# Masked cross attention: the barred keys are added by VectorE in its search for the maximum, GpSimd turns the sign, and the loop is written out

## The reference

```python
q = (layernorm(x) @ wq.T + bq) / sqrt(16);  k = ctx @ wk.T + bk;  v = ctx @ wv.T + bv    # per head: 112 x 16, 375 x 16
last_key = cumsum(steps)                       # per batch, one number for each of the 112 queries
scores = q @ k.T                               # 112 x 375 for each head
scores = where(key_index > last_key, barred, scores)
probs = softmax(scores);  x = x + (probs @ v) @ wo.T + bo
```

## Time and profile before

| | us |
|---|---|
| median of three runs | 3923.49 (3920.95 to 3923.75) |
| the profiled execution | 3921.66, its span 3919.8 |
| TensorE busy in the span | 3269.5 (83%) |
| VectorE, ScalarE, GpSimd busy | 1619.4 (41%), 1577.4 (40%), 1254.9 (32%) |
| DMA | 287.81 MB, 73 GB/s over the span |
| mean granted TensorE clock | 0.92 of full speed |

### The profile page before, as it was taken

The page is one execution under the profiler, slowest core; times in us unless marked ns, Lnnn a source line. Parts: engine busy times, 40 slices in busy tenths (PEclk is TensorE's granted clock), DMA queues, the critical chain, the costliest instruction groups (busy, mean ns, idle before and its releaser), DMA issues. The chain is left out here.

```text
span 3919.8 us, 67890 instructions
## 1 busy us (share of the span) xinstructions
PE 3269.5 (83%) x22398; PEld 2797.8 (71%) x22398; DVE 1619.4 (41%) x3595; ACT 1577.4 (40%) x4385; POOL 1254.9 (32%) x1350
## 2 busy tenths in 40 slices
PE   3899829985978838938999999759599999997998
PEld 2777718873656625627888888748488888886998
DVE  2777720002246530024445444310344444444776
ACT  1555504431235522204555555324255555553222
POOL 0000030002000030034666666510266666664211
PEclk8999959997989958979999999879799999997999
DMA  6555418872100014330000000059300000000101
GB/s 176 129 130 130 97 54 317 310 258 64 35 16 0 0 35 139 113 94 13 9 12 8 8 8 5 3 199 314 115 9 8 8 8 8 8 5 6 33 25 32
DMA packets 155097, 287.81 MB, mean 73 GB/s; under 512 B 53210, under 2 KB 126748, under 8 KB 137116
## 3 DMA queue, kind: packets, MB, share of 16 engines
q1 hardware_dynamic: 147292, 267.81, 22.3%
q0 software_dynamic: 7680, 18.36, 1.8%
HBM read 240.75 MB, written 45.35 MB: 73 GB/s over the span
## 5 line engine op out<-in xcount | busy, mean ns | idle before, releaser
L712 POOL TENSOR_SCALAR L_probs<-L_probs,L_inverse 112x375 f32<-112x375 f32 x512 | 645.2, 1260 | 88.3 <-issue 88.3
L835 DVE TENSOR_REDUCE L_negmax<-bank 112x1 f32<-112x375 f32 x768 | 416.8, 543 | 406.8 <-PE bank L482 337.5
L676 ACT ACTIVATE L_probs<-bank,L_negmax 112x375 f32<-112x375 f32 x768 | 439.5, 572 | 334.0 <-DVE L_negmax L835 332.0
L710 POOL TENSOR_TENSOR L_inverse<-L_sums,neg_one 112x1 f32<-112x1 f32 x512 | 315.2, 616 | 324.1 <-ACT L_probs L676 318.5
L507 PE MATMUL bank<-ident,L_probs 112*125 112x112 f32 x2304 | 372.3, 270 | 10.4 <-POOL L_probs L712 8.6
L507 PEld LDWEIGHTS bank<-ident,L_probs 112*125 112x125 f32 x2304 | 360.1, 189 | 18.6 <-POOL L_probs L712 15.5
L657 ACT ACTIVATE L_probsT<-bank 125x336 f32<-125x336 f32 x512 | 231.3, 452 | 291.4 <-PE bank L507 289.3
L522 PE MATMUL bank<-L_probsT,v 125*64 125x112 f32 x3072 | 206.1, 270 | 1.1 <-ACT L_probsT L657 1.1
L639 ACT ACTIVATE v<-bank 125x512 f32<-125x512 f32 x192 | 114.9, 598 | 197.4 <-PE bank L432 197.4
L478 PE MATMUL bank<-L_keys_hi,L_q_hh 128*112 128x376 f32 x512 | 183.3, 358 | 0.0
L522 PEld LDWEIGHTS bank<-L_probsT,v 125*64 125x64 f32 x3072 | 150.6, 137 | 29.1 <-ACT L_probsT L657 1.6
(11 more groups left out here) (294 smaller groups left out, 7297.3 us busy)
## 6 DMA issues: line engine op xcount, KB each, us to landing
L0t_w<-in_F_w SPq DMA_DIRECT2D x70, 1024.0 KB, 5.1
L2t_w<-in_F_w SPq DMA_DIRECT2D x42, 1024.0 KB, 5.1
L_keys<-spread_k SPq DMA_DIRECT2D x64, 376.0 KB, 6.6
L_ctxT<-in_ctxT SPq DMA_DIRECT2D x48, 375.0 KB, 3.4
L1t_w<-in_F_w SPq DMA_DIRECT2D x16, 1024.0 KB, 6.0
slots_in<-zeros SPq DMA_DIRECT2D x4, 1792.0 KB, 16.5
L_q<-spread_q SPq DMA_DIRECT2D x128, 56.0 KB, 2.2
spread_k<-L_k_hi SPq DMA_DIRECT2D x16, 376.0 KB, 2.5
```

What stands on the lines that cost most here:

```text
L676: act.activation(probs[h % NB][:, :], psS[h % 2][0:T, 0:S], ACT.Exp, bias=negmax[b.par][:, h:h + 1], accum_out=sums[b.par][:, h:h + 1]).th ...
L710: pool.tensor_tensor(inverse[b.par][:, h:h + 1], sums[b.par][:, h:h + 1], core.neg_one[0:T, :], ALU.pow)
L712: pool.tensor_scalar(probs[h % NB][:, :], probs[h % NB][:, :], inverse[b.par][:, h:h + 1], None, ALU.mult)\
L835: dve.tensor_reduce(negmax[b.par][:, h:h + 1], psS[h % 2][0:T, 0:S], AX, ALU.max, negate=True).then_inc(maxed.sem, 1)
```

## The change

For the attention without `wide` only:

- TensorE no longer multiplies identity and `barred`; the score matmul alone fills the bank, and it waits for `maxed` of head h - 2 and not for `exped`. The wait for the barred tile at head 0 is gone.
- VectorE's `head_max` becomes one `tensor_tensor_reduce`: it adds the score bank and `barred`, writes the sum to `probs[h % 4]` in SBUF, and writes the maximum of each row, with its sign as it is, to `maxes`.
- GpSimd has a new step for each head, `negate`: it waits for `maxed`, multiplies the 112 maxima by -1 into `negmax`, and counts `negated`. Its step for the layer norm stands behind the one of head 0.
- ScalarE waits for `negated` in place of `maxed` and reads `probs[h % 4]` (SBUF), in place, in place of the score bank.
- In `run`, batches 1 to 13 are written out one by one for TensorE, ScalarE, VectorE and GpSimd. SyncE's loop stays.
- The semaphore `barred_ready` is gone and `negated` takes its name's place in another stage.

```diff
+            maxes = [sb(f"maxes{i}", [T, H]) for i in range(2)]
+            negated = core.counter("negated")
...
-            with engine.Fori(0, (B - 4) // 2) as i:
-                heads(Batch(i, 1), False, False)
-                heads(Batch(i, 2), False, False)
-            heads(Batch(0, B - 3), False, False)
+            if wide:
+                with engine.Fori(0, (B - 4) // 2) as i:
+                    heads(Batch(i, 1), False, False)
+                    heads(Batch(i, 2), False, False)
+                heads(Batch(0, B - 3), False, False)
+            else:
+                for n in range(1, B - 2):
+                    heads(Batch(0, n), False, False)
...
-                        pe.wait_ge(barred_ready.sem, barred_ready.at(b.n + 1))
-
-                    pe.wait_ge(exped.sem, exped.at(H * b.n + h - 1))
-                    pe.matmul(psS[h % 2][0:T, 0:SP], core.ident_b[0:T, 0:T], barred[b.par][:, :],
-                              start=True, stop=False)
+                    pe.wait_ge(maxed.sem, maxed.at(H * b.n + h - 1))
                     pe.matmul(psS[h % 2][0:T, 0:SP], q4[b.par][:, h, :], keys4[b.par][:, h // 2, :],
-                              start=False, stop=True).then_inc(scored.sem, 1)
+                              start=True, stop=True).then_inc(scored.sem, 1)
...
-                        act.wait_ge(maxed.sem, maxed.at(H * b.n + h + 1))
-                        act.activation(probs[h % NB][:, :], psS[h % 2][0:T, 0:S],
+                        at_max = maxed if wide else negated
+                        act.wait_ge(at_max.sem, at_max.at(H * b.n + h + 1))
+                        act.activation(probs[h % NB][:, :], psS[h % 2][0:T, 0:S] if wide else probs[h % NB][:, :],
...
-                rstd(Batch(0, 0))
-                with pool.Fori(0, B - 1) as i:
-
-                    pool.wait_ge(var_ready.sem, var_ready.at(i + 2))
-                    pool.tensor_tensor(stats[:, 9:10], stats[:, 8:9], core.neg_half[0:T, :], ALU.pow)\
-                        .then_inc(rstd_ready.sem, 1)
+                def negate(b, h):
+
+                    pool.wait_ge(maxed.sem, maxed.at(H * b.n + h + 1))
+                    pool.tensor_scalar(negmax[b.par][:, h:h + 1], maxes[b.par][:, h:h + 1], -1.0, None, ALU.mult)\
+                        .then_inc(negated.sem, 1)
+
+                def negate_heads(b, b_first, b_last, split_next=True):
+                    for h in range(H):
+                        negate(b, h)
+                        if h == 0 and not b_last:
+                            rstd(b + 1)
+
+                run(negate_heads, rstd, None, lambda b: None, pool)
...
                     dve.wait_ge(scored.sem, scored.at(H * b.n + h + 1))
+                    if not wide:
+                        dve.tensor_tensor_reduce(
+                            out=probs[h % NB][:, :], in0=psS[h % 2][0:T, 0:S], in1=barred[b.par][:, 0:S],
+                            scale=1.0, scalar=-3.0e38, op0=ALU.add, op1=ALU.max,
+                            accum_out=maxes[b.par][:, h:h + 1]).then_inc(maxed.sem, 1)
+                        return
```

More of the change, by code:

```diff
@@ L230, in cross_attention @@
             barred = [sb(f"barred{i}", [T, SP], BF16) for i in range(2)]
-            barred_ready = core.counter("barred_ready")
         weights = core.counter("weights")
@@ L759, in bar @@
                     dve.tensor_scalar(barred[b.par][:, :], keys[:, :], last_key[:, bass.ds(b.n, 1)], NEG,
-                                      ALU.is_gt, ALU.mult).then_inc(barred_ready.sem, 1)
+                                      ALU.is_gt, ALU.mult)
                 def take(p, b, at):
@@ L966, in cross_attention @@
                 s.stage_over(B)
+            negated.stage_over(B * H)
             q_here.stage_over(128 * B)
@@ L976, in cross_attention @@
         if mask:
-            barred_ready.stage_over(B)
             setup_done.stage_over(2)
@@ L2005, in self_attention @@
         o, oT = sb("o", [T, D]), sb("oT", [P, DC, T])
-        mask_ready = core.counter("barred_ready")
+        mask_ready = core.counter("negated")
         weights = core.counter("weights")
@@ L2437 @@
            + [f"{m}_{c}" for m in ("made", "taken") for c in "LQKVOYGH"] + [f"gathered{r}" for r in range(8)]
-           + ["qkv_made", "rope_done", "barred_ready", "w_split", "ctx_split", "k_high", "q_split", "weighed", "q_zeroed",
+           + ["qkv_made", "rope_done", "negated", "w_split", "ctx_split", "k_high", "q_split", "weighed", "q_zeroed",
               "raw_ready", "o_turned", "v_zeroed", "k_stored", "q_stored", "keys_here", "q_here"])
```

## The result

The kernel after the change takes 3944.31 us (median of 5 runs) where the kernel before takes 3923.75 beside it: 1.0059 times as long, with a 95% interval of 1.0044 to 1.0074. A second comparison on another occasion gave 1.0054 [1.0039, 1.0068]. So it is about 21 us slower; 16.5 were forecast. The number came out nearly right, but half of it for another reason than the one given, as the rest of this text shows.

What follows compares the result with a forecast made beforehand. Bound by a loop of engine work and DMA per batch: twelve batches losing 1.17 us (14.0), three others 1.4, the last +1, in all +16.5 us, so 3940 us; own range 3929 to 3956, 8 in 10 3921 to 3962.

Steps and rivals of the forecast that it cites:

- The engine leg: From head 0's start to SyncE's first key store: forecast to grow from 5.62 to 6.10 us, bounds 5.5 and 7.1.
- VectorE's step: The add-and-maximum of each head, replacing the 0.54 us maximum: forecast 0.70 us, bounds 0.54 and 0.81.
- GpSimd's step: Sign turn between maximum and exponential: 0.30 us, or 0.42 with both hand-overs where 0.03 stood; bounds 0.22 and 0.74.
- the matmul that goes: TensorE's barred-key matmul in each head: removing it frees 0.17 us, 2.7 a batch, at most 0.4 of it showing.
- The instruction loads: Fetches of written-out code share the DMA engines with the key and query transfers: 1.1 us more per batch in ten batches.
- the DMA leg: From the key store to the last query landing that releases the next head 0: 19.4 us, 20.5 with instruction fetches beside it.
- A batch then takes 6.10 + 20.5 = 26.6 us, bound by the DMA chain: Masked-stage batch: engine part plus DMA part of the loop through key stores and query loads, against 25.43 us before.
- cost that at nothing: SyncE's query stores move back with `q_split` but queue behind key loads: no cost, at most 1 us a batch without that cover.
- The clock: Rival: TensorE's waits near batch starts lower its clock, costing 1.3 us each; batch 27.9 us, total 3959; chance 0.12.
- VectorE as the bound: Rival: VectorE limits the batch if its new operation takes over 1.0 us; total 3955 at 1.1; chance 0.04.
- faster: Rival at the batch start: four bounds at their favourable end, batch 24.5 us, -11 us, total 3913; chance 0.08.
- Loads without harm: Rival: instruction fetches miss the DMA part or are hidden; batch 25.5 us, +3 us in all, total 3927; chance 0.18.

Runs made afterwards that it cites:

- gpsimd_alone: Kernel before with its loop written out, matmul kept, plain maximum on VectorE and sign turned by GpSimd: 13 batches 348.99 us, in all 1.0083 of before.
- sign_folded: Kernel after without GpSimd's negation: query scale and barred tile negated, VectorE takes the minimum, exponential scales by -1; 13 batches 329.1 us, in all 1.0020 of before.
- loop_only: Kernel before with only batches 1 to 13 written out for every engine but SyncE: 13 batches 334.95 us, in all 1.0033 of before.
- gpsimd_padding: Kernel before with 130 idle one-column memsets on GpSimd in each batch, GpSimd's batches written out: 13 batches 342.6 us, in all 1.0033 of before.

## Why the prediction was right in its number and wrong in its mechanism

*The engine leg* came as described, 5.91 to 6.01 us for 6.10. K1's low part starts 5.37 us after head 0 (213.27 - 207.90), 0.38 later than before, where 0.5 was forecast. The terms were each a little off. VectorE's step was 0.54 + 0.08 us, not 0.70: the tile comes free and the row result costs 0.08. GpSimd's took 0.21, not 0.30; with both hand-overs, from the end of the record of 82 ns at 209.02 to the exponential at 209.34, it is 0.32 us, not 0.42. The exponential itself, which now reads SBUF and no bank, went from 0.57 to 0.61, a term that I had left out. And the matmul that goes gave nothing in front of head 0: its maximum starts 0.56 us after the head (208.46 - 207.90), where it was 0.53, because the remaining score matmul's own record is now the longer one. I had moved everything 0.17 forward there.

*The instruction loads* were right in kind: 16 and 9 packets in the ten batches, and the written-out loop alone costs the masked stage 3.6 us in 13 batches. Where a batch does wait for the chain, the DMA leg is 20.9 to 21.1 us (key store to head 0 of batches 3, 6 and 10), in the range of the five batches that I read it from the earlier trace rows; in batches 8 and 11 head 0 starts 19.5 us after the store. But I charged all batches the mean. That mean was also mixed: of its five batches, 2 and 13 end with no DMA wait, so their 19.8 is TensorE's time and not the chain's. And the leg without loads was nearer 19.0 than 19.4: in the steady batches of the kernel before the last landing lies 0.7 to 0.9 us before head 0, so the slack that I put at 0.4 us was about twice that.

*"A batch then takes 6.10 + 20.5 = 26.6 us, bound by the DMA chain"* is the step that failed. A batch took 26.4, but most were bound by TensorE's own side: of the thirteen starts three waited for the chain. I had written that its work "falls towards 25.43 - 2.7 = 22.7 us", by subtracting sixteen barred matmuls from a batch of 25.43. That counted TensorE's instructions and left its waits as they were. In fact its longest waits hang on steps of VectorE and ScalarE behind the very chain that the change makes longer. ScalarE's copy of the transposed rows stands behind the exponentials of four heads, and these behind GpSimd's step: relative to head 0 the copy moved from 215.83 - 207.99 = 7.84 to 216.48 - 207.90 = 8.58 us. TensorE's work fell by 2.1 us a batch at full clock (23.29 to 21.21), not by 2.7, and all of it went into its waits, so that such a batch is 25.42 us still. `gpsimd_alone` shows this with the matmul kept (+0.9 us a batch), and `sign_folded` without the step (batches of 24.7 to 24.8 where nothing else intervenes). The place where I "cost that at nothing", the steps behind the key leg, in the sentence on the query stores, is where this was lost: the DMA queue did hide them, TensorE did not.

*The clock* was a rival, and its mechanism is real, but I had its place wrong. I put it at each start of a batch, behind a DMA wait of 2 us. It fell in the middle, from head 4 on, behind two waits of 1.57 and 0.89 us with 0.9 us of work between them, in eleven of thirteen batches; where no DMA is waited for, such a batch is about 1.0 us longer. At the start of a batch it stayed at 1.00 in these kernels even behind waits of 2.26 us (the second profile after) and 2.83 us (`sign_folded`, batch 1), and fell behind 3.01 (`loop_only`). With the idle matmuls the fall is gone, and the chain of the forecast appears at last, with 26.15 us a batch. The two mechanisms overlap: without the clock's fall 8.6 of the 12 us stay, and without TensorE's instruction loads all of them stay. So either alone would have given much of this number, and that the forecast's mean came within 0.2 us of a batch's length is in part luck.

*VectorE as the bound* and *faster* did not happen. *Loads without harm* was nearer than the forecast: 3.6 us in 13 batches, where I charged 1.1 to each. Its page of the Trainium skill, "Runtime: NRT & Kernel Launch", section "Instruction fetch mechanics", calls the crossing into a new block mostly hidden and prefers written-out code. For the engines' own issue that holds here (with the loop alone written out, the batches that don't wait for a DMA are 25.4 to 25.6 us); beside a DMA chain the loads cost 3.6 us, and no written-out form in this study is faster than the kernel before (1.0033 for the loop alone).

*The sum.* Where +16.5 were forecast, all in the masked stage, that stage holds 9.6: 12.1 in the 13 batches, less 3 us that batches 0 and 1 gained (53.3 us for 56.4 together), where I had +1. Where head 0 of batch 1 had waited 3.39 us and run at a fallen clock, it waited 0.28 and 2.26 us in the two profiles after and took 1.57 us both times, for 3.41 before. Why batch 0 is itself 1.5 us shorter was not followed up. The other 11 to 13 us come from outside the stage, 10 of them in the two expert stages with TensorE written out. I had cost that at nothing without naming it. The miss inside the stage (7 too many) and the omission outside (11 too few) have nearly cancelled, and that is luck.

## What to carry to other kernels

Taking an instruction from the busiest engine gains only as much as that engine's waits don't grow; before subtracting its duration, follow each of its waits to its releaser and ask whether the change lengthens the path there. A hand-over through a third engine costs more than its step (0.21 us of work, +1.1 us a batch over 13 batches in `gpsimd_alone`), because several queues stand behind it and because an emptier stretch can lower the clock; a sign is better folded into constants, which adds no instruction (`sign_folded`: 14.3 us less than the kernel after in the 13 batches, though in all still 1.0020). An engine on which nobody waits is not free either: idle memsets on GpSimd held up a step of VectorE by 0.6 us. And when a form of the code changes, compare every stage of the two traces, not only the one that was edited.

## What the runs showed of the hardware that was not expected

- VectorE adds a bf16 tile to a bank, writes the result and reduces it in 0.542 us for 112 x 375, no longer than the plain reduction (0.543); the row result is 0.082 more.
- ScalarE's exponential of 112 x 375 takes 0.607 us from SBUF and 0.574 from a bank.
- GpSimd's multiplication of one column takes 0.209 us, against 0.616 for its power.
- The granted clock fell to 0.50 for three us after TensorE had been busy for 0.90 of 3.00 us, and in `gpsimd_alone` to 0.72 in the mean of four us after 1.92 of 3.00, with no wait above 1.1 us. A wait of 2.83 us at the start of a batch left it at 1.00 (`sign_folded`). Four idle matmuls at each of two heads kept it at 1.00.
- While 130 memsets of one column ran on GpSimd (4.35 us), a VectorE step of 112 x 256 that takes 0.40 us alone took 0.99, and ended 0.14 us after the last memset (`gpsimd_padding`, ten batches of ten).
- Kernels with TensorE's program written out have two later stages that are together 10 us longer in the mean (seven against seven, the two groups touching), with longer waits for streamed weights. The cause is open.
